# Value products and score products of a windowed-attention layer, each issued in two halves on TensorE

## The chip, the cores and the metric

The kernel runs on one core of one Trainium2 chip. The metric is the time of one execution in microseconds of device time; the text gives the median of three runs. All rows come from one profiled execution.

## The reference

The input is (4, 512, 128) float32. The reference runs `x + 0.5*ffn(layernorm(x))`, then a sigmoid attention with 16 heads of 8, then the first form once more. Each `ffn` is six layers deep, and every layer is a local attention followed by a gated feed-forward. Cut to what matters here:

```python
def local_attention(q, k, v):                 # w = 32, 16 heads of 64
    bk2, bv2 = look(k), look(v)               # each window sees itself and the window before it
    sim = einsum('bhwie,bhwje->bhwij', bq, bk2) * 8.0
    sim = where(mask, -max, sim)
    attn = softmax(sim, -1)
    return einsum('bhwij,bhwje->bhwie', attn, bv2)

def attn_layer(x, Wqkv, qs, ksc, Wo):
    q, k, v = split(x @ Wqkv, 3, -1)
    q, k = l2norm(q) * qs, l2norm(k) * ksc
    ...                                       # rotary, with a scale
    return local_attention(q, k, v) @ Wo

for i in range(6):
    x = attn_layer(shift_tokens(x), Wqkv[i], ...) + x
    x = ffn_layer(shift_tokens(x), ...) + x
```

## The kernel before, in words

The two deep stacks (`stack(0)` and `stack(1)`) take nearly all of the time. Each has 6 layers, a layer has 4 batches, and a batch has 4 tiles of 128 tokens: 96 tiles for a stack, 192 in all. Each engine has a program of its own with an order written out by hand, and the engines meet by semaphores. One call of `step` handles tile T in its first phase, tile T-1 in its second and tile T-2 in its third, so every engine always works on three tiles; the feed-forward of a batch (`f_...`) is spread over the steps s = 0 to 3 of later batches. Since there are 192 tiles, there are 192 full steps, 48 for each s.

A step on TensorE (PE) runs, in order:

- `project` 0 to 3: the q and k projections of tile T (lines 625 to 627), three matmuls each, into the `duo` banks;
- `turn_qk` 0 to 3: transposes of the normalised q and k of tile T-1 (L649), four each;
- `turn_prob`: transposes of the probabilities of tile T-2 (L679), four for each of two parts;
- `outputs`: the value products of tile T-2 (L693), 64 small matmuls, which the profile shows as 128 instructions of 64x32;
- `values` 0 and 1: the v projections of tile T (again lines 625 to 627);
- `scores`: two matmuls that put the mask into `sv` (L659), and then the score products of tile T-1 (L666), 64 small matmuls, shown as 128 of 64x64.

`outputs` and `scores` write the same two PSUM banks, `sv` (`sv_all` in the rows). ScalarE (ACT) copies the value products out of them with `store_out` (`oT`, L887, two instructions), and VectorE (DVE) takes the scores out of them with `shift_max` (L1055 and L1057). So `scores` waits for `act_o` (both copies of `store_out` done) as well as for `act_k` (the fourth `store_qk` of tile T-1, `kT`, L899) and `pool_carry`. ACT's own order in a step is `store_qk` 2, `store_out`, `store_qk` 3, then the norm's logarithm and exponential (L864, L869), then `store_v` 0 and 1 (L860).

After `scores`, DVE subtracts the maximum, ACT takes the exponential (L874), DVE sums and inverts (L1063, L1067), and then DVE (L1071) and GpSimd (POOL, L1178) each normalise one half of the probabilities. `turn_prob` waits for these two, in that order. `turn_qk` waits for POOL's `normalise` (`qkn`, L1172).

The feed-forward steps that stand near the place of the change are: `f_rep` (L728) in s = 0, `f_gate` 2 (L734) and `f_up` 1 (L739) in s = 1, `f_up` 2 (L739) in s = 2, and `f_var` (L720) in s = 3. The part of `step` around the change reads, in the kernel before:

```python
if two:
    outputs(T - 2, ...)
if s == 1 and f2:
    f_gate(B - 2, 2)
if one:
    turn_qk(T - 1, 3, two)
...                        # f_rep, f_up 2 or f_var, by s
if now:
    values(T, q, s, 0)
if s == 1 and f2:
    f_up(B - 2, 1)
if one:
    scores(T - 1, ...)
if now:
    values(T, q, s, 1)
```

Of the kernel before, what the change touches and what calls it, by code (L numbers as in the profile page):

```python
# [12 lines left out]
P = 128  # L13
# [7 lines left out]
PAIRS = HEADS // 2  # L21
TILES = SEQ // P
WPT = P // WIN
KEYS = 2 * WIN
CH = 512
HPC = CH // DH
# [19 lines left out]
def tile_done(T, j=0, per=1):  # L46

    return (T + TILE_LEAD) * per + (j + 1)
# [8 lines left out]
def windows_done(B):  # L57

    return (B + BATCH_LEAD + 1) * (16 * V_DMAS)
# [20 lines left out]
def build(nc, x_in, gWq, gWk, gWv, gWo, Wqkv, q_scale, k_scale, Wo, ln_g, ln_b, W1, b1, W2, b2,  # L80
          rope_in, ident_in, mask_in, slot_in, sel_in, out):
    ctx = ExitStack()
    with ctx:
# [106 lines left out]
        pe_s = tsem("pe_s", 1)  # L190
# [66 lines left out]
        def wait_apart(eng, semaphore, value):  # L257

            eng.wait_ge(semaphore, value)  # L260
            eng.sem_inc(passed[eng], 1)
# [222 lines left out]
        def stack(half):  # L484
# [135 lines left out]
            def pe_program(pe):  # L620
# [28 lines left out]
                        last = pe.transpose(tr[c % 2][:, i * P:(i + 1) * P], qkn[:, 0, c, i * P:(i + 1) * P], ident[:, :])  # L649
                    last.then_inc(pe_tqk, 1)  # L650

                def scores(T, s):

                    p = s % 2
                    pe.wait_ge(act_o, tile_done(T - 1, 1, 2))
                    pe.wait_ge(act_k, tile_done(T, 3, 4))
                    pe.wait_ge(pool_carry, tile_done(T))
                    for par in range(2):
                        pe.matmul(sv[par][:, :], identb[:, :],  # L659
                                  maskb[:, 1 if s == 0 else 0, :].unsqueeze(1).broadcast_to([P, HPC, KEYS]),  # L660
                                  start=True, stop=False, skip_group_check=True)
                    for pair in range(PAIRS):
                        for w in range(WPT):
                            for par in range(2):
                                r = slice(par * DH, (par + 1) * DH)
                                last = pe.matmul(sv[par][w * WIN:(w + 1) * WIN, pair * KEYS:(pair + 1) * KEYS],  # L666
                                                 qT[r, p, pair, w * WIN:(w + 1) * WIN],
                                                 kT[r, p, pair, w * WIN:w * WIN + KEYS],
                                                 start=False, stop=True, skip_group_check=True)
                    last.then_inc(pe_s, 1)  # L670

                def turn_prob(T, p, followed):

# [6 lines left out]
                                                prob[:, p, par, 2 * i:2 * i + 2, :].rearrange("q n k -> q (n k)"), ident[:, :])  # L680
                        last.then_inc(pe_tp, 1)

                def outputs(T, B, s):

                    v = s % 2
                    pe.wait_ge(dve_sub, tile_done(T))
                    pe.wait_ge(act_p, tile_done(T, 1, 2))
                    wait_apart(pe, v_loaded[s], windows_done(B))
                    for j in range(4):
                        for w in range(WPT):  # L690
                            for half_of, par in ((0, 0), (1, 1), (0, 1), (1, 0)):
                                r = slice(half_of * KEYS, (half_of + 1) * KEYS)
                                last = pe.matmul(sv[half_of][par * DH:(par + 1) * DH, j * P + w * WIN:j * P + (w + 1) * WIN],  # L693
                                                 vw[r, v, w, j * P + par * DH:j * P + (par + 1) * DH],
                                                 pT[r, 4 * par + j, w * WIN:(w + 1) * WIN],
                                                 start=True, stop=True, skip_group_check=True)
                    last.then_inc(pe_pv, 1)

                def f_wo(B, L, h, part):

# [56 lines left out]
                def step(span, L, new_layer, B, L_prev, q, s):  # L757

                    T = B * TILES + s
                    now, one, two = span.tile(s, 0), span.tile(s, 1), span.tile(s, 2)  # L760
                    f1, f2 = span.batch(1), span.batch(2)
                    first = span.i == 0
                    if now:
                        if s == 0:
                            pe.wait_ge(pool_lo, batch_done(B))
                        if new_layer:
                            weights_ready(L, first, 0)
                        project(T, q, s, 0)
                    if s == 0 and f1:
                        f_wo(B - 1, L_prev, 0, 0)  # L770
                    if s == 1 and f2:
                        f_gate(B - 2, 0)
                        f_up(B - 2, 0)
                    if s == 2 and f1:
                        f_wo(B - 1, L_prev, 1, 0)
                    if s == 3 and f1:
                        f_mean(B - 1)
                    if now:
                        if new_layer:
                            weights_ready(L, first, 1)  # L780
                        project(T, q, s, 1)
                    if one:
                        turn_qk(T - 1, 0)
                    if s == 0 and f1:
                        f_wo(B - 1, L_prev, 0, 1)
                    if one:
                        turn_qk(T - 1, 1)
                    if s == 2 and f1:
                        f_wo(B - 1, L_prev, 1, 1)
                    if s == 3 and f2:  # L790
                        f_w2(B - 2, f1)
                    if now:
                        if new_layer:
                            weights_ready(L, first, 2)
                        project(T, q, s, 2)
                    if s == 1 and f2:
                        f_gate(B - 2, 1)
                    if two:
                        turn_prob(T - 2, s % 2, one)
                    if now:  # L800
                        if new_layer:
                            weights_ready(L, first, 3)
                        project(T, q, s, 3)
                    if one:
                        turn_qk(T - 1, 2, two)
                    if two:
                        outputs(T - 2, B if s >= 2 else B - 1, (s - 2) % TILES)
                    if s == 1 and f2:
                        f_gate(B - 2, 2)
                    if one:  # L810
                        turn_qk(T - 1, 3, two)
                    if s == 0 and f2:
                        f_rep(B - 2, f1)
                    if s == 2 and f2:
                        f_up(B - 2, 2)
                    if s == 3 and f1:
                        f_var(B - 1)
                    if now:
                        if new_layer:
                            weights_ready(L, first, 4)  # L820
                        values(T, q, s, 0)
                    if s == 1 and f2:
                        f_up(B - 2, 1)
                    if one:
                        scores(T - 1, (s - 1) % TILES)
                    if now:
                        values(T, q, s, 1)

                def body(span, L, B, new_layer, L_prev, q):
                    for s in range(TILES):  # L830
# [777 lines left out]
```

## Time and profile before

| | |
|---|---|
| runs | 3648.79, 3652.70, 3658.39 us; median 3652.7 |
| profiled execution | 3656.53 us, its span 3654.8 us |
| TensorE (PE) matmuls | 3287.4 us busy (90%), 61692 instructions |
| PE weight loads (PEld) | 2149.2 us (59%), 61692 instructions |
| VectorE (DVE) | 2817.2 us (77%) |
| ScalarE (ACT) | 2230.3 us (61%) |
| GpSimd (POOL) | 2340.6 us (64%) |
| granted TensorE clock, mean | 0.961 of full speed |

The busy time of PE counts an instruction from its start to its modelled end; instructions overlap there, so 90% doesn't mean that the array works at its peak. Every fp32 product of the program is recorded as more than one instruction in the small products. An idle time carries the name of what ended it; "issue" stands where the engine waited for nothing that the profile shows. Of PE's idle time, most lies inside or right behind the small products.

### The profile page before, as it was taken

To read this page: it belongs to the slowest core of one execution; us is meant where nothing else is said; L and a number is where in the kernel's file an instruction comes from. 1 tells how busy PE (TensorE), PEld (TensorE's weight loads), DVE (VectorE), ACT (ScalarE), POOL (GpSimd) and SP (SyncE) were. 2 spreads that over 40 slices of the span, in tenths; PEclk is the share of its full clock that TensorE was granted. 3 is DMA by queue.
4 is the path that set the end of the run, shared out by engine and by line. 5 is a ranking of instruction groups with operands and counts; after the bars stand their busy time and mean duration, and the time that the engine had idled before them with its cause. 6 is when DMAs were issued, how large, how long until landed. Compare 5 with 4: busy or idle time off the path is not lost. (4 is left out here: it accounts for less than half of the span.)

```text
span 3654.8 us, 147212 instructions
## 1 busy us (share of the span) xinstructions
PE 3287.4 (90%) x61692; PEld 2149.2 (59%) x61692; DVE 2817.2 (77%) x4178; ACT 2230.3 (61%) x3970; POOL 2340.6 (64%) x2167
## 2 busy tenths in 40 slices
PE   5899999999999999996897899989999999999996
PEld 2566666666666666663223566666666666666664
DVE  4788888887887888882344788877877788888883
ACT  3566676765665666662774566665666566666663
POOL 4677787776776777772003677666666667777761
PEclk8999999999999999997998899999999999999997
DMA  3234334334334333320001233323323333333321
GB/s 118 74 92 112 87 92 117 86 85 115 80 87 112 82 91 97 84 72 18 21 1 31 69 77 93 81 72 92 79 74 92 76 77 94 86 78 96 82 73 32
DMA packets 216859, 289.96 MB, mean 79 GB/s; under 512 B 61068, under 2 KB 105864, under 8 KB 215304
## 3 DMA queue, kind: packets, MB, share of 16 engines
q1 hardware_dynamic: 216200, 280.54, 29.8%
q8 instruction: 491, 8.04, 0.9%
q14 instruction: 168, 1.38, 0.1%
HBM read 43.43 MB, written 10.49 MB: 15 GB/s over the span
## 5 line engine op out<-in xcount | busy, mean ns | idle before, releaser
L1166 POOL TENSOR_TENSOR rot<-t 128x512 f32<-128x512 f32 x768 | 975.1, 1273 | 309.4 <-DVE t L1025 289.7
L1172 POOL TENSOR_TENSOR qkn<-rot,rn 128x512 f32<-128x512 f32 x768 | 793.1, 1043 | 174.7 <-DVE rn L1048 174.7
L1024 DVE TENSOR_TENSOR t<-duo,table 128x512 f32<-128x512 f32 x768 | 526.5, 686 | 156.0 <-ACT sq L854 144.4
L1178 POOL TENSOR_TENSOR prob<-prob,rsum 128x512 f32<-128x512 f32 x192 | 297.0, 1547 | 417.7 <-DVE rsum L1067 417.0
L1025 DVE TENSOR_TENSOR t<-duo,table 128x512 f32<-128x512 f32 x768 | 522.4, 680 | 0.0
L693 PE MATMUL sv_all<-pT,arena 64*64 64x32 f32 x24576 | 419.7, 221 | 82.8 <-issue 82.7
L625 PE MATMUL duo<-w_pair,in_hi 128*128 128x512 f16 x1152 | 452.1, 392 | 34.6 <-POOL in_lo L1193 15.7
L860 ACT ACTIVATE arena<-duo 128x512 f32<-128x512 f32 x384 | 226.8, 591 | 403.5 <-PE duo L627 400.5
L854 ACT ACTIVATE sq<-duo 128x512 f32<-128x512 f32 x768 | 443.7, 600 | 39.9 <-PE duo L627 38.5
L649 PE MATMUL duo<-ident,qkn 128*128 128x128 f32 x3072 | 456.6, 280 | 9.0 <-issue 6.9
L1031 DVE TENSOR_REDUCE n<-sq 128x16 f32<-128x1024 f32 x384 | 464.3, 1209 | 0.0
L693 PEld LDWEIGHTS sv_all<-pT,arena 64*64 64x64 f32 x24576 | 392.0, 136 | 120.9 <-issue 120.6
L626 PE MATMUL duo<-w_pair,in_hi 128*128 128x512 f16 x1152 | 449.8, 390 | 5.1 <-issue 5.1
L627 PE MATMUL duo<-w_pair,in_lo 128*128 128x512 f16 x1152 | 449.3, 390 | 4.9 <-issue 4.9
L649 PEld LDWEIGHTS duo<-ident,qkn 128*128 128x128 f32 x3072 | 370.3, 143 | 125.5 <-issue 41.2
L887 ACT ACTIVATE oT<-sv_all 128x512 f32<-128x512 f32 x384 | 208.4, 594 | 280.7 <-PE sv_all L693 280.7
L666 PE MATMUL sv_all<-kT,qT 64*32 64x64 f32 x24576 | 305.3, 228 | 78.4 <-issue 78.2
L707 PE MATMUL ps<-oT,wo_sb 128*128 128x256 f32 x1536 | 364.8, 380 | 0.8 <-issue 0.8
L666 PEld LDWEIGHTS sv_all<-kT,qT 64*32 64x32 f32 x24576 | 263.0, 106 | 173.6 <-issue 173.3
L880 ACT ACTIVATE pT<-duo 128x512 f32<-128x512 f32 x384 | 212.9, 597 | 228.2 <-PE duo L679 227.5
L1055 DVE TENSOR_REDUCE smax<-sv_all 128x16 f32<-128x1024 f32 x192 | 234.2, 1220 | 134.7 <-PE sv_all L666 134.2
L707 PEld LDWEIGHTS ps<-oT,wo_sb 128*128 128x128 f32 x1536 | 286.0, 191 | 48.1 <-issue 4.8
(125 smaller groups left out, 5002.8 us busy)
## 6 DMA issues: line engine op xcount, KB each, us to landing
arena<-arena SPq DMA_DIRECT2D x1152, 128.0 KB, 2.4
arena<-arena SPq DMA_DIRECT2D x768, 64.0 KB, 2.0
w_pair<-w_split SPq DMA_DIRECT2D x44, 256.0 KB, 4.2
w_stage<-in_L_ffn_Wqkv SPq DMA_DIRECT2D x6, 1536.0 KB, 8.6
w_split<-split SPq DMA_DIRECT2D x30, 256.0 KB, 2.6
wo_sb<-in_L_ffn_Wo SPq DMA_DIRECT2D x12, 512.0 KB, 4.2
xsh<-xs SPq DMA_DIRECT2D x48, 128.0 KB, 2.5
f_in<-xs SPq DMA_DIRECT2D x48, 128.0 KB, 2.2
```

What stands on the lines that cost most here:

```text
L625: pe.matmul(dst, in_hi[:, q, cols], wcols(w_hi), start=True, stop=False)
L626: pe.matmul(dst, in_hi[:, q, cols], wcols(w_lo), start=False, stop=False)
L627: return pe.matmul(dst, in_lo[:, q, cols], wcols(w_hi), start=False, stop=True)
L649: last = pe.transpose(tr[c % 2][:, i * P:(i + 1) * P], qkn[:, 0, c, i * P:(i + 1) * P], ident[:, :])
L666: last = pe.matmul(sv[par][w * WIN:(w + 1) * WIN, pair * KEYS:(pair + 1) * KEYS], qT[r, p, pair, w * WIN:(w + 1) * WIN], kT[r, p, pair, w ...
L693: last = pe.matmul(sv[half_of][par * DH:(par + 1) * DH, j * P + w * WIN:j * P + (w + 1) * WIN], vw[r, v, w, j * P + par * DH:j * P + (par ...
L707: last = pe.matmul(fa[:, 0:2 * P], wo_sb[:, c, :], oT[:, c, cols], start=c == 0, stop=c == PAIRS - 1)
L1024: dve.tensor_tensor(t1[:, b, :].rearrange("p (h d) -> p h d", d=DH), src, cos, ALU.mult)
L1025: dve.tensor_tensor(t2[:, b, :].rearrange("p (h k d) -> p h k d", k=2, d=hd), halves, sin, ALU.mult).then_inc(dve_rot, 1)
L1031: dve.tensor_reduce(n2[:, 2 * h:2 * h + 2, :], sq[:, 2 * h:2 * h + 2, :].rearrange("p c (h d) -> p (c h) d", d=DH), axis=AX.X, op=ALU.add) ...
L1166: pool.tensor_tensor(rot[:, c, :], t1[:, c % 2, :], t2[:, c % 2, :], ALU.add).then_inc(pool_add, 1)
L1172: pool.tensor_tensor(qkn[:, 0, c, :].rearrange("p (h d) -> p h d", d=DH), rot[:, c, :].rearrange("p (h d) -> p h d", d=DH), rn[:, c, :].un ...
```

## The change

`outputs` and `scores` get a parameter `part`, and each call issues one half of the products. The waits of each stay at the start of part 0, and the semaphore that says that the whole is done (`pe_pv`, `pe_s`) is raised at the end of part 1. In `step`, `outputs` part 1 stands behind `turn_qk` 3 and the feed-forward step that follows it, and `values` 1 stands between the two parts of `scores`. Number and shape of the instructions stay as they were, and the programs of ACT, DVE, POOL and the DMA queue keep their order.

```diff
-                def scores(T, s):
+                def scores(T, s, part):
...
+                    if part == 0:
+                        pe.wait_ge(act_o, tile_done(T - 1, 1, 2))
+                        pe.wait_ge(act_k, tile_done(T, 3, 4))
+                        pe.wait_ge(pool_carry, tile_done(T))
...
-                    for pair in range(PAIRS):
+                    for pair in range(PAIRS // 2 * part, PAIRS // 2 * (part + 1)):
...
-                    last.then_inc(pe_s, 1)
+                    if part == 1:
+                        last.then_inc(pe_s, 1)
...
-                def outputs(T, B, s):
+                def outputs(T, B, s, part):
...
-                    for j in range(4):
+                    for j in range(2 * part, 2 * part + 2):
...
-                    last.then_inc(pe_pv, 1)
+                    if part == 1:
+                        last.then_inc(pe_pv, 1)
...
                     if two:
-                        outputs(T - 2, B if s >= 2 else B - 1, (s - 2) % TILES)
+                        outputs(T - 2, B if s >= 2 else B - 1, (s - 2) % TILES, 0)
...
+                    if two:
+                        outputs(T - 2, B if s >= 2 else B - 1, (s - 2) % TILES, 1)
...
                     if one:
-                        scores(T - 1, (s - 1) % TILES)
+                        scores(T - 1, (s - 1) % TILES, 0)
                     if now:
                         values(T, q, s, 1)
+                    if one:
+                        scores(T - 1, (s - 1) % TILES, 1)
```

How the rows of PE's program stand, in a step with s = 2 in the middle of the program. First from the value products (L693) to the score products (L666), before; L649 is `turn_qk` 3, L739 is `f_up` 2, L625 to L627 are `values` 0:

```order
L693 MATMUL sv_all<-pT,arena 64x32 [waits v_loaded0,dve_sub,act_p]
L693 MATMUL sv_all<-pT,arena 64x32 x63
L649 MATMUL duo<-ident,qkn 128x128 [waits pool_qkn,act_p]
L649 MATMUL duo<-ident,qkn 128x128 x3
L739 MATMUL ps<-sqd,w_sb 85x512 [waits dve_hid]
L625 MATMUL duo<-w_pair,in_hi 128x512 [waits dve_rot]
L626 MATMUL duo<-w_pair,in_hi 128x512
L627 MATMUL duo<-w_pair,in_lo 128x512
L659 MATMUL sv_all<-maskb,identb 128x512 [waits pool_carry,act_k,act_o]
L659 MATMUL sv_all<-maskb,identb 128x512
L666 MATMUL sv_all<-kT,qT 32x64 x64
```

The same place with the change (the lines are now L696, L743, L660 and L667):

```order
L696 MATMUL sv_all<-pT,arena 64x32 [waits v_loaded0,dve_sub,act_p]
L696 MATMUL sv_all<-pT,arena 64x32 x31
L649 MATMUL duo<-ident,qkn 128x128 [waits pool_qkn,act_p]
L649 MATMUL duo<-ident,qkn 128x128 x3
L743 MATMUL ps<-sqd,w_sb 85x512 [waits dve_hid]
L696 MATMUL sv_all<-pT,arena 64x32 x32
L625 MATMUL duo<-w_pair,in_hi 128x512 [waits dve_rot]
L626 MATMUL duo<-w_pair,in_hi 128x512
L627 MATMUL duo<-w_pair,in_lo 128x512
L660 MATMUL sv_all<-maskb,identb 128x512 [waits pool_carry,act_k,act_o]
L660 MATMUL sv_all<-maskb,identb 128x512
L667 MATMUL sv_all<-kT,qT 32x64 x32
```

The transposes and the feed-forward step have moved ahead of the second half of the value products, so that only `values` 0 is left between the last value product and the first mask product.

The next rows of PE in the same step, before: the score products, `values` 1, and the first projection of the next tile.

```order
L666 MATMUL sv_all<-kT,qT 32x64 x64
L625 MATMUL duo<-w_pair,in_hi 128x512 [waits dve_rot]
L626 MATMUL duo<-w_pair,in_hi 128x512
L627 MATMUL duo<-w_pair,in_lo 128x512
L625 MATMUL duo<-w_pair,in_hi 128x512 [waits act_v]
```

And with the change:

```order
L667 MATMUL sv_all<-kT,qT 32x64 x32
L625 MATMUL duo<-w_pair,in_hi 128x512 [waits dve_rot]
L626 MATMUL duo<-w_pair,in_hi 128x512
L627 MATMUL duo<-w_pair,in_lo 128x512
L667 MATMUL sv_all<-kT,qT 32x64 x32
L625 MATMUL duo<-w_pair,in_hi 128x512 [waits act_v]
```

`values` 1 now stands in front of the last score product, and so in front of the semaphore `pe_s`.

## Rows read from the trace of the kernel before

**Rows 1.** The page: span, engines, and the instruction queue q8: packets, MB, share.
```profile
span 3654.8 us, 147212 instructions
...
PE 3287.4 (90%) x61692; PEld 2149.2 (59%) x61692; DVE 2817.2 (77%) x4178; ACT 2230.3 (61%) x3970; POOL 2340.6 (64%) x2167
...
q8 instruction: 491, 8.04, 0.9%
```
**Rows 2.** Waits on PE: who waited for whom, us in total, times, longest.
```profile
PE sv_all L693 <- issue: 82.7, 62, 3.4
PE sv_all L666 <- issue: 78.2, 60, 3.1
...
PE sv_all L659 <- ACT oT L887: 4.5, 8, 0.6
```
**Rows 3.** PE's timeline, 999 to 1009 us: start, us, instructions, [idle before <- releaser].
```profile
999.79 1.37 PE L693 MATMUL sv_all<-pT,arena 64*64 64x32 f32 x79
1002.49 0.43 PE L693 MATMUL sv_all<-pT,arena 64*64 64x32 f32 x15 [1.33 <-issue]
...
1006.24 1.19 PE L666 MATMUL sv_all<-kT,qT 64*32 64x64 f32 x99
1008.52 0.45 PE L666 MATMUL sv_all<-kT,qT 64*32 64x64 f32 x29 [1.09 <-issue]
```
**Rows 4.** PE's timeline, 1100 to 1104 us, a step with s = 3.
```profile
1100.46 1.82 PE L693 MATMUL sv_all<-pT,arena 64*64 64x32 f32 x109
1103.04 0.54 PE L693 MATMUL sv_all<-pT,arena 64*64 64x32 f32 x19 [0.76 <-issue]
```
**Rows 5.** PE's timeline, 1017 to 1025 us, a step with s = 2.
```profile
1017.88 2.07 PE L693 MATMUL sv_all<-pT,arena 64*64 64x32 f32 x128
1019.88 0.66 PE L649 MATMUL duo<-ident,qkn 128*128 128x128 f32 x4
1020.37 1.02 PE L739 MATMUL ps<-sqd,w_sb 128*85 128x512 f32 x2
1021.23 0.38 PE L625 MATMUL duo<-w_pair,in_hi 128*128 128x512 f16 x1
...
1021.88 0.59 PE L659 MATMUL sv_all<-maskb,identb 128*128 128x512 bf16 x2
1022.40 1.48 PE L666 MATMUL sv_all<-kT,qT 64*32 64x64 f32 x128
1023.82 0.39 PE L625 MATMUL duo<-w_pair,in_hi 128*128 128x512 f16 x1
```
**Rows 6.** ACT's timeline in the same step.
```profile
1020.08 1.08 ACT L887 ACTIVATE oT<-sv_all 128x512 f32<-128x512 f32 x2 [0.99 <-PE sv_all L693]
1021.05 0.60 ACT L899 ACTIVATE kT<-duo 128x512 f32<-128x512 f32 x1
```
**Rows 7.** PE's timeline, a step with s = 1: `f_up` 1 and the mask product.
```profile
1004.86 1.02 PE L739 MATMUL ps<-sqd,w_sb 128*128 128x512 f32 x2
1005.72 0.59 PE L659 MATMUL sv_all<-maskb,identb 128*128 128x512 bf16 x2
```
**Rows 8.** Timelines of DVE, POOL and PE, after the scores of rows 5.
```profile
1024.41 1.21 DVE L1055 TENSOR_REDUCE smax<-sv_all 128x16 f32<-128x1024 f32 x1
...
1029.59 1.55 POOL L1178 TENSOR_TENSOR prob<-prob,rsum 128x512 f32<-128x512 f32 x1 [1.04 <-DVE rsum L1067]
...
1030.73 1.18 PE L679 MATMUL duo<-ident,prob 128*128 128x128 f32 x8
```
**Rows 9.** All waits: DVE for the scores, us in total, times, longest.
```profile
DVE smax L1055 <- PE sv_all L666: 134.2, 81, 4.7
```
**Rows 10.** POOL's timeline at 1100 us: `normalise` 3, in the step of rows 4.
```profile
1100.99 1.04 POOL L1172 TENSOR_TENSOR qkn<-rot,rn 128x512 f32<-128x512 f32 x1
```
**Rows 11.** The windows view of both stacks; behind POOL's busy time stands the granted clock.
```profile
230.00:1640.00 1410.00, 1317.80 (x26958) 905.80 (x26945) 1205.27 (x1787) 918.52 (x1680) 1039.35 (x964) 0.99 0.36 93
2100.00:3590.00 1490.00, 1380.26 (x28201) 947.72 (x28199) 1237.75 (x1862) 932.30 (x1706) 1049.52 (x974) 0.98 0.33 82
```

More of the change, by code:

```diff
@@ L650, in turn_qk @@
                     last.then_inc(pe_tqk, 1)
-                def scores(T, s):
+                def scores(T, s, part):
                     p = s % 2
[L655 to L661, printed above, removed]
-                    for pair in range(PAIRS):
+                    if part == 0:
+                        pe.wait_ge(act_o, tile_done(T - 1, 1, 2))
+                        pe.wait_ge(act_k, tile_done(T, 3, 4))
+                        pe.wait_ge(pool_carry, tile_done(T))
+                        for par in range(2):
+                            pe.matmul(sv[par][:, :], identb[:, :],
+                                      maskb[:, 1 if s == 0 else 0, :].unsqueeze(1).broadcast_to([P, HPC, KEYS]),
+                                      start=True, stop=False, skip_group_check=True)
+                    for pair in range(PAIRS // 2 * part, PAIRS // 2 * (part + 1)):
                         for w in range(WPT):
@@ L681, in turn_prob @@
                         last.then_inc(pe_tp, 1)
-                def outputs(T, B, s):
+                def outputs(T, B, s, part):
                     v = s % 2
-                    pe.wait_ge(dve_sub, tile_done(T))
-                    pe.wait_ge(act_p, tile_done(T, 1, 2))
-                    wait_apart(pe, v_loaded[s], windows_done(B))
-                    for j in range(4):
+                    if part == 0:
+                        pe.wait_ge(dve_sub, tile_done(T))
+                        pe.wait_ge(act_p, tile_done(T, 1, 2))
+                        wait_apart(pe, v_loaded[s], windows_done(B))
+                    for j in range(2 * part, 2 * part + 2):
                         for w in range(WPT):
```

## The prediction

> **What bounds the kernel now.** I read the page first, then the waits on TensorE (PE), then the timelines of single steps. PE sets the pace: it is busy in 90% of the span [rows 1], and the two stacks together run 192 steps on it. Its largest idle times are not waits for other engines. They are "issue" gaps at the value products and the score products: 82.7 us in 62 gaps and 78.2 us in 60 gaps, 161 us together, 1.3 us each [rows 2]. The timelines show where they lie. A run of value products breaks off after 79 recorded matmuls for 1.33 us, or after 109 for 0.76 us, and a run of score products after 99 for 1.09 us [rows 3, 4]. So a gap comes late in a dense run of 128, never early in the ones that I looked at.
>
> The instruction queue of the page explains it: 491 packets brought 8.04 MB, so 16.4 KB each [rows 1], and with 2 x 61692 matmuls and weight loads one packet holds about 251 of them. A dense run of 128 matmuls with 128 loads uses up a whole packet in 2.00 us (1017.88 to 1019.88) or 1.42 us (1022.40 to 1023.82) [rows 5]. Everything else in a step is far sparser: the three matmuls of a v projection take 0.65 us (1021.23 to 1021.88) [rows 5]. I read the gaps as PE running out of fetched instructions. The change puts sparse work into the dense runs, and that attacks this cause.
>
> But the change also moves the end of the value products and the end of the score products, and both are awaited.
>
> **Term A, the wait in front of the mask products.** The scores overwrite the banks that the value products fill, so the masks wait until ACT has copied both halves out and has then stored the fourth k. In a step with s = 2 the value products end at 1019.88 [rows 5]; ACT starts its two copies at 1020.08 and ends the k store at 1021.65 [rows 6]. With about 0.1 us for the semaphore (an estimate: ACT itself started 0.13 us after the recorded end of the last product, 1019.95), the masks can't start before 1021.75, which is 1.87 us after the value products. Now PE fills this with `turn_qk` 3 (0.49 us), `f_up` 2 (0.86) and `values` 0 (0.65), 2.00 us together [rows 5], so it just fits, and PE waits for ACT here only 4.5 us in the whole run [rows 2]. With the change the first two stand before the second half of the value products. Only 0.65 us is left, and PE waits 1.87 - 0.65 = 1.22 us. The steps with s = 0 and s = 3 have `f_rep` or `f_var` in the same place and lose the same cover. With s = 1, `f_up` 1 stays behind (0.86 us, 1004.86 to 1005.72 [rows 7]), and 0.36 us is left. The sum is 144 x 1.22 + 48 x 0.36 = 193 us. Nothing else is queued on PE that could go ahead. Bounds: 170 us if the semaphore costs nothing and some steps have a stall of PE in just this place, 200 us.
>
> **Term B, the scores end later.** `values` 1 now stands before the last score product, so DVE gets the scores 0.65 us later, counted from the masks. From there a chain runs over DVE, ACT, DVE and POOL to the second part of `turn_prob`. In the step of rows 5 the scores end at 1023.82, DVE starts on them at 1024.41, POOL ends at 1031.14, and PE's second part of `turn_prob` starts some 0.5 us after 1030.73 [rows 8]. So PE has nearly nothing to spare there (0.1 us). DVE was busy until 1024.41, which hides about 0.4 of the 0.65 us; 0.25 is left, less 0.05 of slack. Where DVE already waits for the scores (81 times [rows 9]) nothing is hidden; I take 48 steps of this kind at 0.45 us, since the cover was not equal in all. The sum is 144 x 0.2 + 48 x 0.45 = 50 us. Bounds: 0 if DVE and POOL catch up elsewhere, 100 us if nothing is hidden.
>
> **Term C, `turn_qk` 3 comes earlier.** It moves ahead of half of the value products, 1.0 us. It needs POOL's `normalise` 3. In the s = 3 step at 1100 us POOL ends this at 1102.03 [rows 10]. The value products began at 1100.46 [rows 4], so half of them end at 1101.46, and PE waits 0.6 to 0.7 us. In the other steps the same operation ends more than 1 us ahead, by the timelines. 48 x 0.65 = 31 us; bounds 0 and 35.
>
> **Term D, fewer gaps.** The gaps of rows 2 make 161 us. More of the kind lie right behind a dense run, on other lines; I put those at 50 us, so 210 us in all, about half at each kind of run. Between the halves of the value products there are now 0.49 + 0.86 = 1.35 us of sparse work, which is as long as a mean gap (1.3 us), so I take nine tenths of these gaps away, 95 us. Between the halves of the scores there is only 0.65 us, half a gap: 45 us. Together -140 us. Bounds: -70 (the gaps move rather than go) and -210.
>
> The page "Runtime: NRT & Kernel Launch" of the Trainium skill, section "Instruction fetch mechanics", says that instructions come in 16 KiB blocks of 256, with which the packets here agree, but also that the fetch is hidden because instructions are dispatched more slowly than blocks arrive. By that sentence the gaps would have another cause and term D would be 0; the gaps late in dense runs speak against it. It is the second rival.
>
> **Term E, the clock.** In the two stacks the granted clock is 0.99 and 0.98 [rows 11]. If all of the shortfall were stretches at 1.2 GHz, the lower of its two levels, these would be 2% of 1410 us and 4% of 1490 us, 88 us. They may cost up to half of their length, 44 us. The new wait is as long as a gap and comes in three of four steps, so more such stretches seem likelier than fewer. I take +20 us; bounds -40 and +90.
>
> **The sum.** Against the profiled execution's own 3656.5 us (its span is 3654.8): +193 + 50 + 31 - 140 + 20 = +154, so 3810.5 us. The median of the runs, 3652.7, is 3.8 us lower, so the forecast is 3807 us.
>
> **The rivals.**
> - *Only the wait for the copies is new (chance 0.20).* The later scores and the earlier transposes are hidden because DVE and POOL use PE's new wait to get ahead. For it: both have idle time. Against: the chain of term B starts after that wait. Time: 3652.7 + 193 - 140 = 3706 us.
> - *The gaps stay (chance 0.08).* They are not caused by density, or the halves are still too dense. Time: 3807 + 140 = 3947 us.
> - *Faster after all (chance 0.05).* One mechanism at one place: the sparse work between the halves lets every block of instructions arrive in time, so all 210 us of gaps go, and the low-clock stretches that follow long gaps go with them (40 us), while B and C are hidden. Time: 3652.7 + 193 - 210 - 40 = 3596 us. It decides once the gaps are worth more than the 193 us of term A. Against it: 0.65 us in the scores is half a gap.
> - *Almost no change (chance 0.04).* The same, but the clock stays as it is: 3636 to 3660 us.
> - *The change doesn't do what it says* can be left out: the order of PE's instructions shows it.
>
> **How the numbers follow.** The main case has 0.63. The low end, 3695, takes in the first rival; the high end, 3895, is the main case with D at -70 (+70) and a little from B. Outside are the gaps that stay, the two cases near or below the old time, and the tails. I take 0.3% as what the measurement can tell from no change. Faster by more than that has 0.05, within it 0.03, slower 0.92 (part of the fourth rival's chance falls to "slower").
>
> **What would show it.** In the profile of the changed kernel, PE's wait at the mask product for ACT's copies or k store should be some 190 us, against 4.5 us now. PE's wait at `turn_prob` for POOL should come to some tens of us, and that of `turn_qk` for POOL's `normalise` in s = 3 too. The issue gaps at the value products should nearly vanish, and those at the score products should shrink to half. If the mask product shows no wait, term A is wrong and with it the sign. If the issue gaps keep their 161 us, term D is wrong.

## The result, and the profile after

The changed kernel takes 3836.3 us (median of 4 runs, 3831.5 to 3841.4), the kernel before 3652.0 in the same comparison (median of 4). The ratio is 1.0498, with a 95% interval of 1.0478 to 1.0518, so the change costs 184 us. The forecast was 3807 us, +154. The profiled execution has a span of 3829.7 us.

The waits of the changed kernel, PE's own (who waited for whom, us in total, times, longest):

```profile
PE sv_all L660 <- ACT oT L895: 152.0, 144, 1.8
PE sv_all L667 <- issue: 54.3, 55, 3.0
PE ps L738 <- ACT gel L940: 52.1, 48, 2.8
PE duo L649 <- POOL qkn L1180: 25.3, 45, 0.6
...
PE sv_all L696 <- issue: 9.1, 13, 2.0
...
PE duo L681 <- POOL prob L1186: 5.0, 23, 0.3
```

These answer to [rows 2]. The mask product (now L660) waits for ACT 152.0 us instead of 4.5. "gel" is the result of the gelu, for which the gate products (L738, `f_gate`) wait. The issue gaps at the value products (now L696) went from 82.7 to 9.1 us, those at the score products (now L667) only from 78.2 to 54.3. The page's line of engines shows more PE time, but a smaller share:

```profile
PE 3362.9 (88%) x61692; PEld 2111.0 (55%) x61692; DVE 2796.0 (73%) x4178; ACT 2221.5 (58%) x3970; POOL 2338.9 (61%) x2167
```

The same step as in [rows 5], in PE's timeline with the change:

```profile
1067.56 1.14 PE L696 MATMUL sv_all<-pT,arena 64*64 64x32 f32 x64
1068.63 0.66 PE L649 MATMUL duo<-ident,qkn 128*128 128x128 f32 x4
1069.12 1.02 PE L743 MATMUL ps<-sqd,w_sb 128*85 128x512 f32 x2
1070.07 1.14 PE L696 MATMUL sv_all<-pT,arena 64*64 64x32 f32 x64
1071.14 0.39 PE L625 MATMUL duo<-w_pair,in_hi 128*128 128x512 f16 x1
...
1073.01 0.59 PE L660 MATMUL sv_all<-maskb,identb 128*128 128x512 bf16 x2 [1.05 <-ACT oT L895]
1073.53 0.86 PE L667 MATMUL sv_all<-kT,qT 64*32 64x64 f32 x64
1074.32 0.39 PE L625 MATMUL duo<-w_pair,in_hi 128*128 128x512 f16 x1
...
1075.07 0.86 PE L667 MATMUL sv_all<-kT,qT 64*32 64x64 f32 x64
1075.86 0.39 PE L625 MATMUL duo<-w_pair,in_hi 128*128 128x512 f16 x1
```

And ACT's timeline beside it:

```profile
1071.34 1.08 ACT L895 ACTIVATE oT<-sv_all 128x512 f32<-128x512 f32 x2 [2.68 <-PE sv_all L696]
1072.31 0.60 ACT L907 ACTIVATE kT<-duo 128x512 f32<-128x512 f32 x1
```

The value products end at 1071.14 and the masks start at 1073.01, 1.87 us later. This is the chain of term A to the hundredth: two copies and the k store. It isn't this step alone: the median over the 144 steps with only `values` 0 in between is 1.87 us, and so is that over 44 steps with s = 1, where `f_up` 1 also stands there. In the step shown PE has only `values` 0 in between. The profile names 1.05 us as idle rather than 1.22, since the modelled end of the last matmul lies later than the moment at which the next could start.

The same rows show a price that the prediction doesn't have. The value products, `turn_qk` 3 and `f_up` 2 took 3.35 us in [rows 5] (1017.88 to 1021.23); with the value products in halves they take 3.58 (1067.56 to 1071.14), with no wait among them. The score products and `values` 1 take 2.33 us (1073.53 to 1075.86), where the median of the undisturbed steps of the kernel before is 2.07. So a run that is broken in two is longer by itself, by 0.23 and 0.26 us. Over 192 steps that is an estimated 94 us.

The later scores show on DVE, in the line that answers to [rows 9] (all waits of the changed kernel), and further down the chain on ACT and POOL:

```profile
POOL prob L1186 <- DVE rsum L1075: 578.7, 190, 16.4
...
DVE smax L1063 <- PE sv_all L667: 280.0, 164, 5.6
...
ACT prob L882 <- DVE prob L1065: 190.8, 188, 4.4
```

DVE now waits for the scores 164 times, not 81, so the cover that term B counted on is used up almost everywhere. Term C shows in the s = 3 step that answers to [rows 4, 10], in PE's timeline:

```profile
1084.50 1.14 PE L696 MATMUL sv_all<-pT,arena 64*64 64x32 f32 x64
1086.21 0.63 PE L649 MATMUL duo<-ident,qkn 128*128 128x128 f32 x4 [0.58 <-POOL qkn L1180]
```

The windows view of the two stacks answers to [rows 11]; the granted clock went from 0.99 and 0.98 to 1.00 and 0.99, so it got better. For the whole program the mean granted clock went from 0.961 to 0.978:

```profile
230.00:1740.00 1510.00, 1370.56 (x27256) 900.23 (x27254) 1193.60 (x1798) 923.00 (x1695) 1045.66 (x970) 1.00 0.34 88
2200.00:3760.00 1560.00, 1406.19 (x27754) 923.14 (x27752) 1219.07 (x1841) 917.92 (x1688) 1037.70 (x963) 0.99 0.31 78
```

### The profile page after: what moved, and what is told of

The parts are those of the page before. It is cut to its first block and busy times, and to the rows that moved or that the text cites. A ratio compares the mean times of both kernels' runs of the same rounds, so it can differ in the third digit from the quotient of the medians.

```text
span 3829.7 us, 147212 instructions
## 1 busy us (share of the span) xinstructions
PE 3362.9 (88%) x61692; PEld 2111.0 (55%) x61692; DVE 2796.0 (73%) x4178; ACT 2221.5 (58%) x3970; POOL 2338.9 (61%) x2167
## 5 line engine op out<-in xcount | busy, mean ns | idle before, releaser
L625 PE MATMUL duo<-w_pair,in_hi 128*128 128x512 f16 x1152 | 449.1, 390 | 34.6 <-DVE t L1033 17.0
L649 PE MATMUL duo<-ident,qkn 128*128 128x128 f32 x3072 | 448.3, 276 | 25.4 <-POOL qkn L1180 25.3
L696 PEld LDWEIGHTS sv_all<-pT,arena 64*64 64x64 f32 x24576 | 398.5, 135 | 125.9 <-issue 125.0
L696 PE MATMUL sv_all<-pT,arena 64*64 64x32 f32 x24576 | 442.9, 221 | 9.6 <-issue 9.1
L626 PE MATMUL duo<-w_pair,in_hi 128*128 128x512 f16 x1152 | 442.9, 384 | 1.1 <-issue 1.1
L627 PE MATMUL duo<-w_pair,in_lo 128*128 128x512 f16 x1152 | 442.7, 384 | 0.8 <-issue 0.7
L649 PEld LDWEIGHTS duo<-ident,qkn 128*128 128x128 f32 x3072 | 366.3, 142 | 139.1 <-issue 57.0
L667 PEld LDWEIGHTS sv_all<-kT,qT 64*32 64x32 f32 x24576 | 272.2, 106 | 226.2 <-issue 226.2
L667 PE MATMUL sv_all<-kT,qT 64*32 64x64 f32 x24576 | 342.8, 225 | 54.3 <-issue 54.3
L888 ACT ACTIVATE pT<-duo 128x512 f32<-128x512 f32 x384 | 224.1, 599 | 214.2 <-PE duo L681 203.6
L882 ACT ACTIVATE prob<-prob 128x1024 f32<-128x1024 f32 x192 | 203.4, 1059 | 190.8 <-DVE prob L1065 190.8
```

Source lines behind the costliest of these rows:

```text
L625: pe.matmul(dst, in_hi[:, q, cols], wcols(w_hi), start=True, stop=False)
L626: pe.matmul(dst, in_hi[:, q, cols], wcols(w_lo), start=False, stop=False)
L627: return pe.matmul(dst, in_lo[:, q, cols], wcols(w_hi), start=False, stop=True)
```

## The experiments

Ratios are against the kernel before on the same chip, with 95% intervals; microseconds of a difference are the ratio less 1 times 3652.

**Each half of the change alone.** The edit takes the `part` calls of the scores together again:

```diff
                     if one:
                         scores(T - 1, (s - 1) % TILES, 0)
+                        scores(T - 1, (s - 1) % TILES, 1)
                     if now:
                         values(T, q, s, 1)
-                    if one:
-                        scores(T - 1, (s - 1) % TILES, 1)
```

> Only the value products are in halves; the score products are whole again, with values 1 behind them. My theory (the wait for ACT's copies is 193 us, the earlier transposes 30 us, the gaps saved at the value products about 100 us, the later scores not in it): 3652 + 120 = 3775 us, with the wait of the mask product for ACT as in the changed kernel and the one of the second gate product for its gelu back near its 27 us. The rival (the later scores carry most of the 184 us): below 3660 us.

Measured: 3804.5 us, ratio 1.0386 (1.0361 to 1.0410), +141 us. The mask product waits 147.7 us for ACT in 140 cases, and the gate product is back at 22.3 us. The mechanism of my theory stands, though the time is 21 us more than its +120, and the rival falls. One thing is off: the issue gaps at the whole score products rose to 91.6 us, and this was not foreseen.

The other half alone puts the value products together again:

```diff
                     if two:
                         outputs(T - 2, B if s >= 2 else B - 1, (s - 2) % TILES, 0)
+                        outputs(T - 2, B if s >= 2 else B - 1, (s - 2) % TILES, 1)
...
-                    if two:
-                        outputs(T - 2, B if s >= 2 else B - 1, (s - 2) % TILES, 1)
```

> Only the score products are in halves, with values 1 between them; the value products are whole. My theory: the later scores cost 50 us at turn_prob and some 25 us at the gate product, and the gaps at the score products give 25 to 45 us back: 3675 to 3700 us, and no wait of the mask product for ACT. The rival (the later scores carry most of it): 3800 us or more.

Measured: 3697.7 us, ratio 1.0085 (1.0065 to 1.0106), +31 us, as expected. PE's waits in this kernel:

```profile
PE sv_all L696 <- issue: 74.5, 61, 3.2
PE ps L738 <- ACT gel L939: 54.1, 48, 3.7
PE sv_all L667 <- issue: 48.2, 54, 3.0
```

The gate product (L738) waits 54.1 us for its gelu. In the kernel before, from which this one differs only by the scores, it was 27.3. In ACT's order this gelu stands behind the exponential, and the exponential waits for DVE and so for the scores. These 31 us aren't the later scores alone. The broken run costs 0.26 us in each step (an estimated 50 us), the gate product 27 us more and the first projection (L625, for DVE) 7 us more, and all the issue gaps of PE together shrink by 55 us, from 195.7 to 140.5. The wait for POOL at `turn_prob` only went from 3.1 to 6.0 us, where I had expected 50. The two halves cost 141 + 31 = 172 of the 184 us, so they add up nearly.

**The chain of term A.** ACT stores the fourth k before it copies the value products; the rest is the changed kernel:

```diff
-                    if two:
-                        store_out(T - 2, B if s >= 2 else B - 1, (s - 2) % TILES)
                     if one:
                         store_qk(T - 1, (s - 1) % TILES, 3)
+                    if two:
+                        store_out(T - 2, B if s >= 2 else B - 1, (s - 2) % TILES)
```

> The changed kernel, but ACT stores the fourth k before it copies the value products out, instead of behind them. My theory: the chain from the last value product to the mask product gets shorter by one copy (0.48 us), so the wait goes from 1.22 to 0.74 us in each step with s = 0, 2 and 3 and from 0.36 to 0 with s = 1: 86 us less than the changed kernel, 3750 us. The rival (PE's idle time at the mask products is a restart of a dense run, or a lack of instructions, and not this chain): no change against 3836 us.

Measured: 3685.6 us, ratio 1.0059 (1.0040 to 1.0078). This is 160 us less than the changed kernel (1.0498 - 1.0059), twice what I expected. PE's waits:

```profile
PE sv_all L660 <- ACT oT L895: 72.8, 140, 1.3
...
PE sv_all L667 <- issue: 4.6, 4, 2.9
```

The wait for ACT fell by 79 us, which is the expected 0.5 us a step. But the issue gaps at the score products, which no instruction of PE had been moved to help, fell from 54.3 to 4.6 us. That is taken up below.

The same edit with only the value products in halves:

> Only the value products are in halves, and ACT stores the fourth k before the two copies. My theory: the mask product still waits 0.74 us for the second copy in three of four steps (some 100 us with what PE's weight loads show), the gaps at the value products stay small, and those of the score products are those of before: 3690 to 3720 us where the kernel before has 3660, about 100 us below the run with the halves of the value products alone. The rival (the k store's place matters only while the scores are in halves): 3800 us.

Measured: 3612.8 us, ratio 0.9872 (0.9852 to 0.9893), 47 us faster than the kernel before and 188 us better than without the edit (1.0386). The wait for ACT is 73.1 us in 141 cases, as expected; the gaps at the whole score products are 23.3 us, against 91.6 without the edit. Again the second effect was missing in my theory.

**What the issue gaps are.** The kernel before, with PE's program moved by half a packet:

```diff
                 pe.wait_ge(init_act, 3)
+                for _ in range(32):
+                    pe.matmul(ps[6][:, 0:32], ident[:, :], ident[:, 0:32], start=True, stop=True)
```

> The kernel before, with 32 small fp32 matmuls added at the start of PE's program (128 instructions with their weight loads, half of one fetched packet). If the gaps come from fetched packets, every gap moves: a run that broke off after about 99 recorded matmuls at 1006 us no longer breaks there, and runs that were whole break late instead; the time stays within 0.5% of 3652 us, and the issue gaps stay at 140 to 180 us. The rival (the gaps belong to certain steps, by data or by the work around them): the same runs break at the same places.

Three steps in a row in PE's timeline. In the kernel before the first breaks off twice [rows 3], the second is whole [rows 5], and the third breaks off at 113 and at 94:

```profile
1032.93 1.87 PE L693 MATMUL sv_all<-pT,arena 64*64 64x32 f32 x113
1036.05 0.43 PE L693 MATMUL sv_all<-pT,arena 64*64 64x32 f32 x15 [1.25 <-issue]
...
1039.65 1.60 PE L666 MATMUL sv_all<-kT,qT 64*32 64x64 f32 x94
1041.59 0.51 PE L666 MATMUL sv_all<-kT,qT 64*32 64x64 f32 x34 [0.34 <-issue]
```

The same three steps with the shift:

```profile
1038.60 2.07 PE L695 MATMUL sv_all<-pT,arena 64*64 64x32 f32 x128
...
1044.00 1.48 PE L668 MATMUL sv_all<-kT,qT 64*32 64x64 f32 x128
...
1054.40 1.82 PE L695 MATMUL sv_all<-pT,arena 64*64 64x32 f32 x108
...
1057.90 0.70 PE L695 MATMUL sv_all<-pT,arena 64*64 64x32 f32 x20 [1.68 <-issue]
...
1073.13 2.07 PE L695 MATMUL sv_all<-pT,arena 64*64 64x32 f32 x128
...
1077.60 1.48 PE L668 MATMUL sv_all<-kT,qT 64*32 64x64 f32 x128
```

The broken steps became whole and the whole one broke: the gaps belong to a position in the instruction stream. The rival falls.

The whole traces say the same.
The time came out at 3691.0 us, ratio 1.0075 (1.0049 to 1.0101), a little outside of the expected 0.5%, and the issue gaps at the two dense runs rose from 161 to 185.5 us, also more than expected. So the place of the blocks alone is worth 0.75% here, and this bounds how far any small difference in these gaps can be read.

**Two ways to keep the cover.** First, halves by bank, so that one bank can be copied while PE fills the other:

```diff
-                    for j in range(2 * part, 2 * part + 2):
+                    for j in range(4):
                         for w in range(WPT):
-                            for half_of, par in ((0, 0), (1, 1), (0, 1), (1, 0)):
+                            for half_of, par in ((part, 0), (part, 1)):
```

(Not shown: the scores are whole, and in ACT's order the fourth k is stored between the two copies, each of which waits for its own half.)

> Only the value products are in halves, but each half fills one of the two banks, and ACT copies the first bank out while PE works on the second, then stores the fourth k, then copies the second bank. My theory: only one copy is left behind the last value product, so the chain to the mask product is 0.83 us, of which values 0 covers 0.65; the wait all but goes (0.2 us in a step) and the gaps saved at the value products remain: 3590 to 3630 us where the kernel before has 3660. The rival (products that use one half of the array's rows in turn run slower than the interleaved ones): the value products take more than their 2.0 us for 128 and the time is 3660 us or more.

Measured: 3907.0 us, ratio 1.0674 (1.0650 to 1.0697), +246 us. PE's timeline, the same step:

```profile
1087.23 2.06 PE L697 MATMUL sv_all<-pT,arena 64*64 64x32 f32 x64
...
1090.66 2.06 PE L697 MATMUL sv_all<-pT,arena 64*64 64x32 f32 x64
1092.65 0.39 PE L626 MATMUL duo<-w_pair,in_hi 128*128 128x512 f16 x1
...
1093.42 0.61 PE L661 MATMUL sv_all<-maskb,identb 128*128 128x512 bf16 x2
```

Both mechanisms show, but the forecast of 3590 to 3630 us missed. The masks follow 0.77 us behind the last value product, so all but 0.12 us of the wait is gone. But 64 products now take 1.99 us (1090.66 to 1092.65), where they took 1.07 in the changed kernel (1070.07 to 1071.14). The rival decides: such products, one behind another, run at little more than half the pace of those that alternate. Its reason isn't shown, though. In the kernel before, each product has another half of the array's rows than the one ahead of it and also another PSUM bank; here both stay the same for 64 instructions. No run changes one of the two alone.

Second, only `turn_qk` 3 between the halves, the other feed-forward step behind the second half, steps with s = 3 left whole, scores whole, and the fourth k stored first where s is not 3:

```diff
+                    if two and s == 3:
+                        outputs(T - 2, B if s >= 2 else B - 1, (s - 2) % TILES, 1)
...
                     if one:
                         turn_qk(T - 1, 3, two)
+                    if two and s != 3:
+                        outputs(T - 2, B if s >= 2 else B - 1, (s - 2) % TILES, 1)
                     if s == 0 and f2:
                         f_rep(B - 2, f1)
...
-                    if two:
-                        outputs(T - 2, B if s >= 2 else B - 1, (s - 2) % TILES, 1)
...
+                    if one and s != 3:
+                        store_qk(T - 1, (s - 1) % TILES, 3)
                     if two:
                         store_out(T - 2, B if s >= 2 else B - 1, (s - 2) % TILES)
-                    if one:
+                    if one and s == 3:
                         store_qk(T - 1, (s - 1) % TILES, 3)
```

> Only the value products are in halves, and not in steps with s = 3; between the halves stands turn_qk 3 alone (with the third gate product in s = 1), the other feed-forward step stays behind the second half, and in these steps ACT stores the fourth k first. My theory: behind the last value product PE has 1.51 us of other work against a chain of 1.39 us, so the mask product doesn't wait; the gaps at the value products shrink by a third to a half: 3625 to 3650 us where the kernel before has 3660. The rival (any splitting costs by itself): 3670 us or more.

Measured: 3575.0 us, ratio 0.9773 (0.9752 to 0.9794), 83 us faster than the kernel before, more than I expected. PE's wait for ACT at the mask product is 4.6 us in 10 cases, as in the kernel before, and the gaps went from 82.7 to 46.1 and from 78.2 to 34.5 us:

```profile
PE sv_all L696 <- issue: 46.1, 51, 3.8
PE sv_all L667 <- issue: 34.5, 39, 2.9
```

The rival isn't wrong in kind: splitting does cost by itself, about 0.3 us in steps with s = 0 and 2 (from the value products to `values` 0, 3.35 us whole and 3.64 to 3.68 in halves). The gaps saved are worth more: all of PE's issue gaps together went from 195.7 to 101.6 us.

**The surprise: gaps that follow the waits.** Storing the fourth k first changes which semaphore reaches PE last. So I changed only the order in which PE asks:

```diff
-                    pe.wait_ge(act_o, tile_done(T - 1, 1, 2))
                     pe.wait_ge(act_k, tile_done(T, 3, 4))
                     pe.wait_ge(pool_carry, tile_done(T))
+                    pe.wait_ge(act_o, tile_done(T - 1, 1, 2))
```

> The changed kernel, but PE asks for the three semaphores in front of the mask product in another order: the fourth k and the carry first, ACT's copies last, where they were first. All three are still asked for before the same instruction. The open question: storing the fourth k first also took away the issue gaps at the score products (54.3 us in 55 gaps became 4.6 us in 4), which my theory had left as they were. Theory a (PE's sequencer is held twice, by the copies and 0.48 us later by the fourth k, and the fetch of the next packet starts only after that): with one hold instead of two the gaps at the score products fall to below 20 us and the time by 40 to 70 us, to 3770 to 3800 us. Theory b (what counts is how long PE is held, or what ACT and the DMA do at the time): gaps and time stay, 3836 us within 0.4%.

Measured: 3814.9 us, ratio 1.0448 (1.0426 to 1.0469), 18 us less than the changed kernel, with 37.2 us of gaps at the score products against 54.3. It lies between the two theories.

> The kernel before, with the same other order of the three waits. Theory a: the issue gaps at the score products (78.2 us) shrink by half or more, 3600 to 3630 us where the kernel before has 3657. Theory b: nothing changes, within 0.4%.

Measured: 3613.8 us, ratio 0.9892 (0.9869 to 0.9914), 39 us faster than the kernel before by the order of two waits. PE's waits:

```profile
PE sv_all L693 <- issue: 89.3, 65, 3.7
...
PE sv_all L666 <- issue: 43.9, 41, 3.2
```

Those at the score products went from 78.2 to 43.9 us, and those at the value products, where nothing was changed, stayed near theirs (82.7 and 89.3). Theory a had this number, but by luck: its mechanism fails in the next run and in the traces below.

> The fastest kernel so far (the value products in halves around turn_qk 3 alone, not with s = 3, and the fourth k stored first) with the same other order of the three waits. Here the copies come last already in three of four steps. Theory a: at most 10 to 20 us less than its 3575 us, from the steps with s = 3. Theory b: the same time within 0.4%.

Measured: 3641.3 us, ratio 0.9959 (0.9941 to 0.9977), still below the kernel before but 68 us worse than with the other order, and the gaps at the score products went from 34.5 to 83.7 us. Both theories miss. In this kernel the copies come last, and asking for them last means that PE is held once too. So the number of holds, theory a, isn't what decides. What fits all four is the place of the hold: asking first for what comes last is good. The next run takes this apart, in the kernel before:

```diff
+                    pe.wait_ge(pool_carry, tile_done(T))
+                    pe.wait_ge(act_k, tile_done(T, 3, 4))
                     pe.wait_ge(act_o, tile_done(T - 1, 1, 2))
-                    pe.wait_ge(act_k, tile_done(T, 3, 4))
-                    pe.wait_ge(pool_carry, tile_done(T))
```

> The kernel before, asking first for the carry (there 10 us or more before it is needed), then for the fourth k (the last to arrive), then for the copies (0.48 us before it). Theory c (PE must be held at the first wait of the three; a wait in front of it, even one long met, takes the gain away): gaps at the score products near 78 us and a time within 0.4% of the kernel before. Theory d (a wait long met costs nothing; what matters is that PE is held once and at nothing behind it): near 44 us of gaps and 3614 us, as with the fourth k first, 1.1% less than the kernel before.

Measured: 3657.2 us, ratio 1.0005 (0.9994 to 1.0016), and PE's waits:

```profile
PE sv_all L666 <- issue: 78.4, 56, 3.6
```

That is the kernel before again. What theory c foresaw came true: a wait that is long met, asked for in front of the one that holds PE, takes the whole gain away.

Its line in the source view (duration in ns, shortest/median/longest) in the kernel before, with the fourth k asked first, and with the carry first:

```profile
L657 PEldq EVENT_SEMAPHORE  x192: 51/1926/3417, 74.7 to 3584.3; - x192
...
L657 PEldq EVENT_SEMAPHORE  x192: 51/51/51, 72.9 to 3543.8; - x192
...
L657 PEldq EVENT_SEMAPHORE  x192: 51/496/2322, 74.5 to 3596.4; - x192
```

In the kernel before, the instruction holds the carry and the fourth k, and it ends 0.03 us (median) after the fourth k has come. With the carry first it holds the copies and the fourth k, and again ends 0.03 us after the fourth k; its 0.50 us is the time between the two. With the fourth k first it holds the copies and the carry, ends 0.08 us after the copies, and the mask's weight load then waits 0.45 us for the fourth k by itself. So theory a's picture was the wrong way round: PE is held once in the kernel before, and twice in the faster one. What all of these kernels agree on is where the semaphore that arrives last sits. On the weight load the gaps at the score products are smaller (43.9 against 78.2 us, 34.5 against 83.7, 37.2 against 54.3) than in the separate instruction. Storing the fourth k first makes the copies come last, and these sit on the weight load, so the same reading covers 4.6 against 54.3 and 23.3 against 91.6 us, where ACT's order was changed too.

Last, the best arrangement with the order chosen by step:

```diff
+                        asked = [(act_o, tile_done(T - 1, 1, 2)), (act_k, tile_done(T, 3, 4))]
+                        for need in (asked[::-1] if s == 2 else asked):
+                            pe.wait_ge(*need)
```

(`s` in `scores` is that of tile T-1, so 2 means a step with s = 3.)

> The fastest kernel so far (3575 us), with the order of the waits chosen by step: the semaphore that arrives last is asked for first, so the copies first with s = 0, 1, 2 and the fourth k first with s = 3. If asking first for what comes last is what saves gaps at the score products (78.2 us to 43.9 us in the kernel before), a quarter of the steps gains it here: 34.5 us of gaps become about 25, and the time 3560 to 3572 us where the kernel before has 3655. The rival (its 34.5 us have nothing to do with the steps with s = 3): the same time within 0.3%.

Measured: 3568.0 us, ratio 0.9764 (0.9749 to 0.9779); 29.2 us of gaps at the score products in 43. The sign is as expected, but its interval overlaps with that of the run without it (0.9773, 0.9752 to 0.9794), so a gain over that kernel isn't shown. It is the fastest kernel of the study, 2.4% below the kernel before.

## Why the prediction was right

- **Term A (193 us)** was right in its mechanism and its size. The chain is 1.87 us in the rows, the profile names 152.0 us in 144 cases (1.05 us each, where the chain gives 1.22), and one copy less in it takes 79 us away. It carries the sign.
- **Term B (50 us)** was wrong in its place. At `turn_prob` POOL's half is waited for only 5.0 us by name (3.1 before). The later scores came up elsewhere: 25 us at the gate product, behind a gelu that stands behind the exponential in ACT's order (27.3 us before, 52.1 after), and 7 us at the first projection (9.8 to 17.0). I had followed the chain to one consumer. That the scores in halves cost 31 us doesn't confirm the term, since some 50 of what they cost is the broken run itself, and their saved gaps are in it too.
- **Term C (31 us)** is 25.3 us in 45 cases.
- **Term D (-140 us)** is about -130 in all: PE's issue gaps together were 195.7 us before and are 74.3 after, of which 8.6 stand at the mask product (L660) in 45 cases and are what is left of the wait in steps with s = 1. By place: the value products went from 82.7 to 9.1 us, the score products from 78.2 only to 54.3, where half was expected to go, and those on other lines, which I had put at 50 us, from 34.8 to 2.5.
- **Term E (+20 us)** had the wrong sign: the granted clock rose, though PE waited 1.2 us in three of four steps. From its mean (0.961 and 0.978) the time at the lower level is about 285 us before and 169 after, so up to half of the difference, 58 us, was given back (an estimate). Fewer long gaps came with fewer slow stretches here; the run by bank had few gaps too (4.6 and 5.3 us at the two kinds of product) and a lower clock (0.94), so the gaps alone don't set it.
- **The missing term** is the price of breaking a run in two, 0.23 and 0.26 us in a step, an estimated 94 us. The sum had nothing for it.
- So that the sum was only 30 us too low is in part luck. By the spans the change costs 175 us. The terms as measured make 193 + 25 + 25 + 7 + 94 - 130 = 214 us, less up to 58 us for the clock. The missing price and the wrong sign of the clock nearly cancel (94 us against 78).
- The page "Runtime: NRT & Kernel Launch", section "Instruction fetch mechanics", of the Trainium skill holds the fetch for hidden. The gaps that move with half a packet of added instructions disagree, and the place of the blocks alone changed the time by 0.75%. So the second rival, with term D at 0, falls.

Open is why the gaps depend on where the last semaphore sits. The packets' times give a hint: in the 1 us ahead of the first mask product of a step, 15 packets start in the kernel before and 27 with the fourth k asked first; in the fastest kernel but one it is 52, and with the other order 12. So fetches start later where PE's sequencer stands at a separate instruction. But in the changed kernel and its run with the other order the counts are 8 and 9, though the gaps fell from 54.3 to 37.2 us, so this isn't the whole account. Also open is a version in which ACT copies the first columns of both banks early: TensorE would be writing the same banks at that time, and it wasn't tried.

## What to carry to other kernels

Before work is moved into a dense run, look at what stands behind the run's last instruction: if a reader on another engine hands a buffer back, the work behind the run was its cover, and the split must leave at least that chain's length (here 1.87 us) behind the end. Put a price on the split itself too (here about 0.25 us for each run that was broken). Shorten the chain first (a store that doesn't depend on the run goes ahead of the copies), and then split: the same split cost 3.9% without this and gained 1.3% with it. Where an engine asks for several semaphores in front of one instruction, look at which of them sits on the instruction itself. Here it is the one that the program asks for first, and the kernels were faster when that was the one that arrives last.
